# A two-layer MetaFormer on one core: token norm in one product, register loads in groups of four, and the last convolution unit sent group by group

## The reference, cut to what matters

```
qkv = conv1x1(channel_norm(x), w_qkv)                  # 384 channels
agg = conv1x1(conv5x5(qkv, w_dw, groups=384), w_pw, groups=48)
# heads from qkv and from agg: q, k through relu, linear attention, projection, batch norm; x += that
t      = token_norm(x) as rows (2048, 128)
logits = t @ gate.T                                    # E = 8, then E = 16
top-2 experts per token, softmax of the two logits
out    = sum over the two experts of weight * mlp_e(t)  # 128-512-128 with gelu, then 128-256-128 gated with silu
x += out
```

## Time and profile before

| what | value |
|---|---|
| median of three runs | 468.22 us (463.9 to 469.77) |
| profiled execution, its span | 468.1 us, 466.0 us |
| TensorE busy | 398.7 us, 86% of the span |
| VectorE, ScalarE, POOL busy | 237.1, 189.9, 191.6 us |
| granted TensorE clock, mean | 0.906 |
| up products, line 1316 | 103.0 us in 688 pieces |
| down products, line 1333 | 70.3 us in 500 pieces |
| convolution products, line 1207 | 58.9 us in 480 pieces |

### The profile page before, as it was taken

One profiled execution on the slowest core, in us unless ns is written; L12 is line 12 of the kernel. 1 busy time (PEld: TensorE's weight loads), 2 busy tenths in 40 slices (PEclk: granted clock), 3 DMA queues, 4 the chain that ended last, 5 costly groups with the idle time before them and its releaser, 6 DMA issues.

```text
span 466.0 us, 8714 instructions
## 1 busy us (share of the span) xinstructions
PE 398.7 (86%) x2635; PEld 336.5 (72%) x2635; DVE 237.1 (51%) x584; ACT 189.9 (41%) x441; POOL 191.6 (41%) x206
## 2 busy tenths in 40 slices
PE   7996999999788969999999399898894889888823
PEld 4565999999576838999999254675663888887822
DVE  3604444561254525656666283574672555565615
ACT  4495223223121275777566173563152233222104
POOL 9952344460003037777754200001107775555530
PEclk9997999999979967999999797999865899999985
DMA  4032253442376036981100420000021211110126
GB/s 148 1 69 44 46 86 64 81 81 33 43 230 179 1 109 188 276 239 52 47 36 34 138 66 1 1 0 2 0 89 42 56 50 39 42 42 35 42 87 211
DMA packets 44019, 35.32 MB, mean 76 GB/s; under 512 B 3800, under 2 KB 39752, under 8 KB 43976
## 3 DMA queue, kind: packets, MB, share of 16 engines
q1 hardware_dynamic: 36208, 24.60, 19.9%
q0 software_dynamic: 4096, 8.40, 5.8%
q10 hardware_dynamic: 3672, 1.77, 2.5%
HBM read 21.12 MB, written 7.34 MB: 61 GB/s over the span
## 4 chain that ended last, share of the span: by engine, by line
PE 65%; DVE 10%; ACT 8%; issue 6%; DMA 5%; DVEq 3%; ACTq 1%; POOL 1%; SPq 0%; POOLq 0%
PE bank L1316 15%; PE bank L1207 11%; PE bank L1333 8%; PE bank L1166 3%; DVE w_block L951 2%; PE bank L1060 2%; DMA ln_sq<-y 2%; PE bank L1359 2%; ACT heads L543 2%; DVEq L947 2%; PE bank L1241 2%; PE bank L1253 2%; PE bank L1077 2%; PE bank L1245 1%; PE bank L1260 1%
## 5 line engine op out<-in xcount | busy, mean ns | idle before, releaser
L1316 PE MATMUL bank<-x_cols,w_block 128*128 (+1 forms) x688 | 103.0, 295 | 15.7 <-DVE w_block L951 10.9
L1316 PEld LDWEIGHTS bank<-x_cols,w_block 128*128 128x128 f32 x688 | 88.2, 201 | 26.2 <-issue 24.3
L482 POOL DMA_INDIRECT x_rows<-tok,token x64 | 62.1, 970 | 60.8 <-DMA tok<-ln_sq 41.6
L489 POOL DMA_INDIRECT y<-wide,dest x64 | 62.5, 977 | 46.1 <-DVE wide L983 40.3
L1333 PE MATMUL bank<-w_down,h_cols 128*128 (+1 forms) x500 | 70.3, 277 | 0.8 <-DVE wide L983 0.8
L1333 PEld LDWEIGHTS bank<-w_down,h_cols 128*128 128x128 f32 x500 | 62.9, 193 | 1.2 <-DVE h_cols L966 0.7
L1207 PE MATMUL bank<-cmap,cw 128*128 128x112 f32 (+2 forms) x480 | 58.9, 280 | 0.3 <-DVE router_c L793 0.3
L1207 PEld LDWEIGHTS bank<-cmap,cw 128*128 128x128 f32 x480 | 57.4, 198 | 0.4 <-DVE router_c L793 0.4
L312 POOL TENSOR_TENSOR cw<-pw_in,dw_band 128x640 f32<-128x640 f32 x24 | 37.2, 1571 | 44.1 <-PE bank L1207 38.4
L476 POOL MEMSET wide<- 128x4096 f32 x2 | 7.0, 3512 | 105.4 <-DVE xs L1034 63.7
L958 DVE TENSOR_TENSOR h_in<-bank,wT 128x512 f32<-128x512 f32 x39 | 27.0, 692 | 30.4 <-PE bank L1316 19.7
(11 more groups left out here) (209 smaller groups left out, 630.2 us busy)
## 6 DMA issues: line engine op xcount, KB each, us to landing
cmap<-heads SPq DMA_DIRECT2D x48, 64.0 KB
w_up<-in_L_ffn_w_dram SPq DMA_DIRECT2D x1, 2048.0 KB, 8.6
tok<-ln_sq SPq DMA_DIRECT2D x8, 256.0 KB, 2.2
w_up<-in_L_ffn_gate_w_dram SPq DMA_DIRECT2D x4, 512.0 KB
w_up<-in_L_ffn_up_w_dram SPq DMA_DIRECT2D x4, 512.0 KB
w_down<-in_L_ffn_down_w_dram SPq DMA_DIRECT2D x4, 512.0 KB
wide<-y SPq DMA_DIRECT2D x8, 256.0 KB, 4.2
ln_sq<-y SPq DMA_DIRECT2D x8, 256.0 KB, 4.6
```

Source lines behind the costliest of these rows:

```text
L482: pool.indirect_dma_start(out=x_rows[:, j % RING, :], out_offset=None, in_=tok_dram[r], in_offset=bass.IndirectOffsetOnAxis(ap=token[r][:, ...
L489: pool.indirect_dma_start(out=y_dram[r], in_=y_acc[:, s * C:(s + 1) * C], in_offset=None, out_offset=bass.IndirectOffsetOnAxis(ap=dest[r][ ...
L1316: mm = pe.matmul(bank[2 + j % 2][:, i * 128:(i + 1) * 128], w_block[:, j % 3, i * 128:(i + 1) * 128], x_cols[:, bass.ds((j - e[j]) * 128, ...
```

## The change

It has three parts, and the diff shows them.

**Token norm.** `router_c` is replaced by `tok_w`, which holds for each layer the centring matrix and the centred router weights side by side (128 + E columns), filled by VectorE at step 2 of the convolution. TensorE makes, per tile, one product that gives the centred row and its logits, three tiles to a bank, 16 products in six groups (`ROW_GROUPS`); the separate products for logits, columns, rows and variances are gone. ScalarE copies each group's logits to `tok_lg` in SBUF, takes each tile's square with a running sum over its 128 columns (`accum_out`, into `tok_ss`), and the root of eight sums at once. VectorE's router waits for the six copies of the logits and reads them in `tok_lg`. Two `keep_clock` products stand behind the row products; the inverse map goes to bank 0.

**Register loads.** The table `items` holds two rows per layer: the expert of each item, and its block number times 128, clamped. `item_load` reads up to four values (`LOADS`) with one call, without the run-time bounds check. VectorE and TensorE read both tables, ScalarE that of the experts. The block's table adds a step for VectorE in the router, and one step leaves `item_masks`.

**The last convolution unit.** Each group of unit 11 has its own `conv_mm`, its groups go to banks 1, 0, 1, 0, and group 0 waits until unit 10 has been copied (before, unit 9 was enough). ScalarE copies it group by group; SP sends groups 0 to 2 whole and the first half of group 3, ScalarE the second half. The three early projection products go in the order 2, 1, 0.

```diff
+LAST = len(UNITS) - 1
+CONV_SENT = [16 * GU * len(UNITS) // 2 + (16 if i == LAST % 2 else 0) for i in range(2)]
+LOADS = 4
+EXPERT, BLOCK = 0, 1
...
-        def conv_send(queue, u, i):
+        def conv_send(queue, u, i, part=0, parts=1):
             t, v = UNITS[u]
-            g = v * GU + i
-            queue.dma_start(heads_agg[t][G8 * g:G8 * (g + 1), :, :, :].rearrange("p x y b -> p x (y b)"),
-                            conv_out[:, u % 2, i, :]).then_inc(conv_sent[u % 2], 16)
+            n = G8 // parts
+            a = G8 * (v * GU + i) + n * part
+            queue.dma_start(heads_agg[t][a:a + n, :, :, :].rearrange("p x y b -> p x (y b)"),
+                            conv_out[n * part * HW:n * (part + 1) * HW, u % 2, i, :]).then_inc(conv_sent[u % 2], 16)
...
+        def item_load(engine, which, r, what, n, NI, most):
+            k = min(LOADS, NI - n)
+            return engine_values(which, items[r][0:1, what, n:n + k], most)
+        def engine_values(which, table, most):
+            return nc.values_load_multi_w_load_instructions(
+                table, engines=(which,), min_val=0, max_val=most,
+                skip_runtime_bounds_check_because=IN_BOUNDS)[1]
+        ROW_BANKS = ((4, 5, 6, 7, 2, 3), (4, 5, 6, 2, 7, 3))
+        def row_tile(r, i):
+            n = C + (E0, E1)[r]
+            return bank[ROW_BANKS[r][i // 3]][:, (i % 3) * n:(i % 3 + 1) * n]
+        ROW_GROUPS = [range(3 * g, min(3 * g + 3, TT)) for g in range(6)]
...
+            for i in range(GU):
+                sp.wait_ge(conv_copied, LAST + 1 + i)
+                conv_send(sp, LAST, i, 0, 2 if i == GU - 1 else 1)
+            sp.wait_ge(conv_mm, LAST + GU)
...
+                if u == LAST:
+                    i = s % GU
+                    act.wait_ge(conv_mm, LAST + 1 + i)
+                    act.activation(conv_out[:, LAST % 2, i, :], bank[(LAST + i) % 2][:, i * 128:(i + 1) * 128],
+                                   ACT.Relu if UNITS[LAST][0] == 0 else ACT.Copy).then_inc(conv_copied, 1)
+                    if i == GU - 1:
+                        act.wait_ge(conv_copied, LAST + GU)
+                        conv_send(act, LAST, i, 1, 2)
...
+                def squares(tiles):
+                    for i in tiles:
+                        act.activation(ln_sq[:, i * 128:(i + 1) * 128], row_tile(r, i)[:, 0:C], ACT.Square,
+                                       accum_out=tok_ss[:, i:i + 1]).then_inc(tok_sqd, 1)
+                def roots(h):
+                    act.wait_ge(tok_sqd, TT * r + 8 * h + 8)
+                    act.activation(tok_std[:, 8 * h:8 * h + 8], tok_ss[:, 8 * h:8 * h + 8], ACT.Sqrt,
+                                   scale=1.0 / C, bias=eps[:, 1:2]).then_inc(tok_root, 1)
+                for g, tiles in enumerate(ROW_GROUPS):
+                    act.wait_ge(rows_mm, 6 * r + g + 1)
+                    a, n = tiles[0], len(tiles)
+                    src = bank[ROW_BANKS[r][g]][:, 0:n * (C + E)].rearrange("p (t q) -> p t q", t=n)
+                    act.activation(tok_lg[:, a:a + n, 0:E], src[:, :, C:C + E], ACT.Copy).then_inc(tok_logits, 1)
+                    if g < 4:
+                        squares(tiles)
+                    if g == 3:
+                        roots(0)
+                squares(range(12, TT))
+                roots(1)
...
-                        e = act.value_load(expert[r][0:1, n:n + 1], min_val=max(0, n - NB + 1), max_val=min(E - 1, n))
+                        if n % LOADS == 0:
+                            es = item_load(act, mybir.EngineType.Activation, r, EXPERT, n, NI, E - 1)
+                        e = es[n % LOADS]
...
-                    dve.tensor_copy(router_c[:, :], bank[7][:, 0:E0 + E1]).then_inc(router_out, 1)
+                    dve.tensor_copy(tok_w[:, 0, C:C + E0], bank[7][:, 0:E0])
+                    dve.tensor_copy(tok_w[:, 1, C:C + E1], bank[7][:, E0:E0 + E1]).then_inc(router_out, 1)
+                    for i in range(2):
+                        dve.tensor_copy(tok_w[:, i, 0:C], center[:, :]).then_inc(router_out, 1)
...
-                dve.wait_ge(rt_mm, NCH * (r + 1))
+                dve.wait_ge(tok_logits, 6 * (r + 1))
...
+                dve.tensor_copy(items[r][:, EXPERT, 0:NI], item[0:1, 0, 0:NI]).then_inc(rt_table, 1)
+                step(dve.tensor_tensor(b_f, item_id[:, 0:NI], e_f, ALU.subtract))
+                dve.tensor_scalar(items[r][:, BLOCK, 0:NI], item[0:1, 1, 0:NI], float(NB - 1), 128.0, ALU.min, ALU.mult)\
+                    .then_inc(rt_table, 1)
...
+                    if j % LOADS == 0:
+                        for i, v in enumerate(item_load(dve, mybir.EngineType.DVE, r, EXPERT, j, NI, E - 1)):
+                            e[j + i] = v
...
+                        if j % LOADS == 0:
+                            for i, v in enumerate(item_load(dve, mybir.EngineType.DVE, r, BLOCK, j, NI, (NB - 1) * C)):
+                                at[j + i] = v
-                        acc = y_acc[:, bass.ds((j - ej) * C, C)]
+                        acc = y_acc[:, bass.ds(at.pop(j), C)]
...
+                elif u == LAST:
+                    pe.wait_ge(conv_copied, LAST + max(0, i - 1))
+                b = u % 2 if u < LAST else (LAST + i) % 2
...
+                pe.wait_ge(router_out, 3)
+                for g, tiles in enumerate(ROW_GROUPS):
+                    for i in tiles:
+                        if i % 4 == 0:
+                            pe.wait_ge(*ready(i // 4))
+                        mm = pe.matmul(row_tile(r, i), xs[:, i * 128:(i + 1) * 128], tok_w[:, r, 0:C + E],
+                                       start=True, stop=True)
+                    mm.then_inc(rows_mm, 1)
+                keep_clock(0, 2)
+                slots(r, E)
...
-                                           x_cols[:, bass.ds((j - e[j]) * 128, 128)],
+                                           x_cols[:, bass.ds(at[j], 128)],
```

More of the change, by code:

```diff
@@ L169, in metaformer @@
         token = [sb(f"token{r}", [128, NB], I32) for r in range(2)]
-        expert = [sb(f"expert{r}", [1, NI], I32) for r, NI in enumerate((NI0, NI1))]
+        items = [sb(f"items{r}", [1, 2, NI1 + 1], I32) for r in range(2)]
         place_of = sb("place_of", [128, NB], I32)
@@ L316, in build_weights @@
                 ALU.mult).then_inc(cw_built[i % 2], 1)
+        IN_BOUNDS = "experts are counts of E - 1 comparisons, and a block is an item's number less its expert, kept in range"
+        def item_load(engine, which, r, what, n, NI, most):
[10 more added lines that the diff above has]
+        ROW_GROUPS = [range(3 * g, min(3 * g + 3, TT)) for g in range(6)]
         def chunk(t, c, n=CH):
@@ L602, in token_scales @@
             def token_scales(r):
+                E = (E0, E1)[r]
                 load_table(ACT.Sqrt)
-                for c in (0, 1, None, 2, 3):
-                    if c is not None:
-                        act.wait_ge(tok_cent, NCH * r + c + 1)
-                        act.activation(chunk(ln_sq, c), bank[3][:, :], ACT.Square).then_inc(tok_sqd, 1)
-                    if c in (None, 3):
-                        h = 0 if c is None else 1
-                        act.wait_ge(tok_var, NCH * r + 2 * h + 2)
-                        act.activation(tok_std[:, 8 * h:8 * h + 8], bank[3 * h][:, 256 + 8 * h:256 + 8 * h + 8],
-                                       ACT.Sqrt, bias=eps[:, 1:2]).then_inc(tok_root, 1)
+                def squares(tiles):
[17 more added lines that the diff above has]
+                roots(1)
             def router_exp(r):
@@ L842, in router @@
                 oh1, oh2 = (hots[:, k, :, 0:E] for k in range(2))
-                lg = bank[0][:, 0:TT * E].rearrange("p (t e) -> p t e", e=E)
+                lg = tok_lg[:, :, 0:E]
                 m1, m2, d = (rv[:, i, :] for i in range(3))
@@ L1287, in slots @@
                 mm.then_inc(rt_prefix, 1)
-                between()
-                pe.wait_ge(tok_root, 2 * r + 1)
                 pe.wait_ge(rt_value, r + 1)
@@ L1309, in moe_tensor @@
                         j = n - 1
-                        e[j] = pe.value_load(expert[r][0:1, j:j + 1], min_val=max(0, j - NB + 1), max_val=min(E - 1, j))
+                        if j % LOADS == 0:
+                            for i, v in enumerate(item_load(pe, mybir.EngineType.PE, r, BLOCK, j, NI, (NB - 1) * 128)):
+                                at[j + i] = v
                         pe.wait_ge(m.w, j + 1)
@@ L1327, in moe_tensor @@
                         j = n - 3
+                        if j % LOADS == 0:
+                            for i, v in enumerate(item_load(pe, mybir.EngineType.PE, r, EXPERT, j, NI, E - 1)):
+                                e[j + i] = v
                         ej = e.pop(j)
```

89 lines of the change are left out of this document (33 added, 56 removed).

## The result

The changed kernel took 447.44 us, median of four runs (444.86 to 449.81); the kernel before took 468.96, median of its four. The ratio is 0.9554, 95% interval 0.9498 to 0.961: faster by 4.5%. The profiled execution took 449.81 us with a span of 448.1 us and a mean granted clock of 0.895. The forecast was 449.

The account below looks back on a forecast made before the run. TensorE was the bound on average (65% of the chain of waits), but not in the hand-over, routers and expert loops. -3.9 - 1.9 - 2.5 - 4.8 - 6.0 + 0.2 = -18.9 against 468.1 gave 449 us, range 441 to 464.

Parts of the forecast that it names:

- Hand-over, wait: After the last convolution unit: TensorE's wait for its transfers ends 2.9 us earlier, idling 1.5 instead of 4.4 us.
- Hand-over, clock: Behind that wait: TensorE's granted clock stays at 2.4 GHz instead of 1.2, 1.0 us more (bounds 0 and 2.5).
- Routers: The two routers, with the new token norm: -1.9 us in the first, about -2.5 us in the second.
- VectorE's later start: In the routers: ScalarE's logit copies and squares delay VectorE's first step, by 2.8 us in the first, about 2.6 in the second.
- the cap of -2.5 by VectorE's token numbers: Second router: VectorE's token numbers, with two more table steps of 0.2, limit a gain of -3.1 or so to about -2.5.
- Layer 0: First expert loop: TensorE becomes the bound at about 1.80 us per item instead of 1.98; -4.8 us over 34 items.
- Layer 1: Second expert loop: 1.63 us per item instead of 1.79 through fewer register loads; -6.0 us over 41 items.
- L: Price of one four-value register load in the expert loops, taken as 0.41 us, bounds 0.30 and 1.2.
- 0.52 us gap: Second expert loop: VectorE's gap between sum and weight copy, once in two items, which an item without a load closes.
- rival 2: Expert loops: a grouped load is four loads in a row (L = 1.2), +9.7 and +4.5 us, 474 us; chance 0.07.
- rival 1: Expert loops: each word of a load costs most of a load's price (L near 0.9), 462 us; chance 0.20.
- Rival 3: Expert loops end on ScalarE or the gathers, half of both loops' gain lost: 455 us, or 457; chance 0.28.

Follow-up runs that it names:

- e1_conv: The kernel before with only the last convolution unit sent group by group; ratio 0.998 to the kernel before (interval 0.9938 to 1.0023).
- e3_norm: The kernel before with only the token norm part of the change; 464.56 us, ratio 0.9839 to the kernel before.
- e10_bounds: The changed kernel with one value per register load and the bounds check put back; 486.16 us, ratio 1.0385 to the kernel before.
- e9_again2: The changed kernel run again unedited, on another chip; 448.94 us, ratio 0.9572 to the kernel before.
- e4_again: The changed kernel run once more, unedited; 448.06 us, ratio 0.9533 to the kernel before.
- e5b_loads1: The changed kernel with one value per register load, still unchecked; 479.49 us, ratio 0.9679 to the kernel before; on another chip 452.68 us, 0.9676.
- e8b_logits: The changed kernel with eight of a router's twelve squares behind the logit copies; 479.11 us, ratio 0.9683 to the kernel before; on another chip 443.18 us, 0.9488.

## Why the prediction was right, and where its steps were not

The time came out within 2 us and the case was the forecast's: all three parts cut the stretches that they were meant to cut, and TensorE became the bound of layer 0's loop. That it came out so close is in part luck, as the end of this section shows. Its steps, each against its term:

- **Hand-over, wait: right.** -2.9 forecast; -2.6 measured in the whole, -2.5 alone (e1_conv). Alone it gave the time back in the router behind it.
- **Hand-over, clock: wrong.** The step "so I let it stay at 2.4 GHz" was wrong in the trace of the result. It was drawn from a clock that was still 1.00 within the wait; it was so again, and fell behind it. Its 1.0 us was wrong in every case: a clock that holds is worth 0.2 to 0.4 us.
- **Routers: both terms were mis-sized, -1.9 and -2.5 where -4.1 and -3.7 came out** (e3_norm: -4.1 and -3.9). The step that failed is VectorE's later start. I had 12 squares at 0.34 us and seven small steps at 0.2, and so +2.8 and +2.6 us. A square with its accumulator read takes 0.26 us in a row of them (0.77 for three), below my lower bound of 0.27, and a logit copy in such a row 0.08. VectorE starts 4.6 us behind the first row product where it started 3.5 behind the first logit product, and in the second router 4.8 where it was 3.5: +1.1 and +1.3. In the first router I also left out VectorE's first wait, 1.12 us for the counts, of which 0.44 remain: "TensorE loses the separate logit, centering and variance products: that costs or saves nothing" is false by these 0.7 us. The other two waits were given back as forecast. So the second reciprocal comes 14.5 us behind the first row product, where it came 17.0 behind the first logit product, and not unmoved; that half of the row copies stand behind it and no longer all, -2.1, was right. In the second router the cap of -2.5 by VectorE's token numbers did not bind: the store of the rows ends last there too.
- **Layer 0: right.** TensorE is the bound from the fourth item on, and from the 22nd at 1.79 us per item (forecast 1.80); -4.7 against -4.8.
- **Layer 1: right in mechanism, the load's price a little high.** L is 0.34, not 0.41; ahead of the weight copy the load shows 0.17 us, not 0.31, and ahead of the sum 0.16, not 0.26. So 1.56 us per item in place of 1.63, and -7.1 against -6.0 (0.15 x 41 is 6.2, not 6.0).
- **The check.** I set its loss into the same 0.52 us gap as the load and gave it no term. With two tables it is the larger part: 29.1 us of the 34.5 by which e10_bounds' loops are longer than e9_again2's. What it was in the kernel before, with one table, no run tells apart.
- **Rivals 1 and 2** fall with L = 0.34. (The second loop's +9.7 in rival 2 is 9.4 by its own numbers, and the first loop's -1.0 in rival 1 is -0.5; neither moves its time by 1 us.) The Trainium skill, page "Runtime: NRT & Kernel Launch", section "Instruction fetch mechanics", has about 200 ns per register even in bulk, said of HBM; by that an estimate for a four-value load is 0.8 us; the prediction's 0.9 does not follow from it. From these tables in SBUF it is 342 ns against 306 for one, 12 ns for each further register, so the rule does not carry over. Whether it holds for HBM no run here shows.
- **Rival 3:** in part true. In layer 1 of the result's trace the loop ends on the gathers for 16 us of its first 21 items, and one late landing costs 1.2 us; in e4_again and e9_again2 it doesn't. It is far from the half of both loops' gain that the rival put on it. No loop ended on ScalarE in the stretches read.

The total is better than its terms: the touched stretches gave 22.4 us, 3.5 more than the 18.9 forecast, and the untouched ones took back 4.2, of which 5.5 is a start that the same kernel also does in 39.26 us. That the two nearly cancel is luck. A single pair of profiled executions carries some 5 us of that kind either way.

## What to carry to other kernels

Before writing that work taken from an engine "saves nothing", list every wait that ends on it in the stretch, and follow each back: VectorE had three in the old router, 4.3 us together, and all three ended on what TensorE made. Price a row of small instructions by their distance in a row and not by the duration of one: that was worth 1.7 and 1.3 us of the two routers here. Price the sequencer's instructions together, by how far they outlast the array instruction ahead of them: a register load here fitted under it, the bounds check behind the load mostly did not, and a check per value and per table cost more than the grouping of loads saved. When a loop gets faster, look at which engine now ends last in each part of it. A part that gains nothing alone, as the hand-over did, should be judged by its own stretch and by the chain that follows it.

## What the runs showed of the hardware

- VectorE's TENSOR_LOAD from SBUF takes 306 ns for one register and 342 for four; TensorE's 300 and 331, ScalarE's 278 and 310. The longest take up to 0.9 us.
- The bounds check of a loaded value takes VectorE 183 to 190 ns and 23 for the assertion, ScalarE and TensorE about 151 and 18. Behind a load that runs under an instruction of 0.35 us all of it showed on VectorE, behind one of 0.42 us up to half of it was covered.
- Twelve squares of 128x128 with running sums pass ScalarE at 0.26 us each, read of the accumulator included; three logit copies of 128x24 among them take 0.08 each.
- The same instructions at the start of the same program were granted 1.00 in one execution and 0.50 in another, worth 5 us (39.26 and 44.24). The same attention took 62.10 us at a mean clock of 0.95 and 65.81 at 0.87.
- One chip ran the kernel before in 497.57 us instead of 469.9, with the excess of the kernels profiled there in the expert loops (98 to 101 us each; e5b_loads1 and e8b_logits took 80 to 90 on another chip). In e5b_loads1 it lay where the gathers ran.
